# First layer of batch 0: weight halves ahead of x in the load queue, masked half 0 applied ahead of half 1's products

## The chip, the cores and the metric

One NeuronCore of a Trainium2 chip. The metric is device time in microseconds of one execution. The kernel before was timed in three runs: median 412.96 us, 412.57 to 413.46.

## The reference

Four sequences (batches) of 512 tokens with 256 features go through two layers with residuals.

```python
# layer 0: weights mixed per batch by cond (4 x 8), masked, applied
masked_w = weight * mask[None]                       # weight 8 x 256 x 256
w_bot = einsum('bg,got->bot', cond, masked_w)
x = x + einsum('bnt,bot->bno', x, w_bot) + bias
# layer 1: top 2 of 8 experts by softmax(cond), and a shared expert, each a gated MLP 256 -> 1024 -> 256
mlp(x) = (gelu(x @ gate) * (x @ up)) @ down
x = x + mlp_shared(x) + sum_k w_k * mlp_expert_k(x)
```

## The kernel before

Everything is held transposed: features on the 128 partitions (two halves, hh or oh), tokens along the free axis. Products of full precision are made from fp32r operands split in two: hi = the rounded value (a ScalarE copy), lo = the rest (a subtraction on VectorE or GpSimd, called POOL here), and three matmuls hi*hi, hi*lo, lo*hi.

A batch has 24 steps. Step s is one chunk of 128 hidden features: gate and up projection (`gate_up`, `project`, L524 to L562: twelve matmuls of 512 columns), then GELU on ScalarE (`activate`), the product on VectorE (`form_h`, L1044), and the splits of that. Two steps form a pair, whose down projection is done with seven block products instead of eight (L582); its operands are sums and differences t1 to t4 (`form_t1`, `form_t234`) and B12, copied on ScalarE (`copy_b12`). Steps 0 to 7 use the shared expert, 8 to 23 the two chosen ones. TensorE runs two steps ahead: while VectorE works on step s it projects step s + 2. The up projection of step s + 2 goes to the PSUM buffer of step s, so it waits for `split_b11` or the t parts of it (L557 to L562): for step 2 it waits until `h_lo_done` is 1, which is the first `split_b11` (L1080) behind the second `form_h`.

Ahead of that stands the prologue, in which batch 0 gets its first layer. The masked weights of an output half oh are a sum over g of cond[g] times l0_raw[:, oh, g]. Part of the eight products is made by VectorE (`combine_0`, L971, into l0_first), part by TensorE with a diagonal matrix holding cond[g] (`mix_l0`, L426, into PSUM; a plain fp32 matmul, recorded as two passes). VectorE adds the two (`add_mixed_0`, L980, and for half 1 `add_mixed_1`, L990, in two parts th), multiplies by the mask (L985, L996), ScalarE makes the hi part (L694, L698), VectorE the lo part (L1001, L1005). x enters p_ps through an identity matmul (`pass_x` with its hi part, `pass_x_rest` with its lo part), so that p_ps holds x plus the first layer; `first_layer_part` (L443) adds the weights' matmuls. When an output half of p_ps is complete (`l0_done`), ScalarE forms x1_hi (`first_x1_hi`, L755), VectorE x1_lo (`first_x1_lo`, L1014), and ScalarE later x1 itself (`first_x1`, L759). `keep_warm` (L651) issues matmuls on zeros.

The order of the work on every engine is written out by hand, at the end of its block: TensorE L660 to L681, ScalarE L891 to L926, VectorE L1190 to L1218, POOL in its `batch_0`, and SP's queue, which issues all loads, from L409. Engines run in their own order and wait for semaphores. On POOL, `batch_0` starts when half 1 is masked (`first_masked` at 3), then splits the first shared gate and up weights one after the other, then forms sums of the down weights (`form_s`, the last of its four at L1252), splits chunk 3 (L1233) and the down weights (L1262, L1264). Routing weights (`route_sums`, `route_weigh` at L957: a reciprocal L959, a tensor_tensor L961, a tensor_scalar L963, a scalar_tensor_tensor L965, all on 4 or 8 columns, each waiting for the one before) are VectorE's, between the splits of half 1 and the rests of x1.

The order of the loads is: weights 0 to 3 of half 0 (512 KB), all of x of batch 0 (512 KB), weights 4 to 7 of half 0, the mask with the bias (257 KB), weights 0 to 3 of half 1, weights 4, 5 and 6, 7 of half 1 (256 KB each), then the shared expert's weights.

Of the kernel before, what the change touches and what calls it, by code (L numbers as in the profile page):

```python
# [10 lines left out]
ACT = mybir.ActivationFunctionType  # L11
# [23 lines left out]
def build(nc, xT, cond, l0_w, l0_mask, experts, shared, outT):  # L35
# [22 lines left out]
    with ExitStack() as ctx:  # L58
# [90 lines left out]
        l0_in = [sem(f"l0_in{i}") for i in range(5)]  # L149
        mask_in = sem("mask_in")  # L150
        first_mixed = sem("first_mixed")
# [50 lines left out]

        DIAGS = (2, 3, 6, 7, 5)

# [52 lines left out]
        def chunks_at(s):  # L257

            if s == 1:
                return range(4, 5)  # L260
            if s == 3:
                return range(5, 7)
            if s == 5:
                return range(7, 10)
            return range(s + 3, min(s + 5, CHUNKS + ECH))
# [4 lines left out]
        def _(sp):  # L270
# [7 lines left out]
            def load_l0_last(i):  # L278
                at = slice(QUAD + 2 * i, QUAD + 2 * (i + 1))
                sp.dma_start(l0_raw[:, 1, at], l0_w[1, 1, :, bass.ds(2 * i * D, 2 * D)].rearrange("p (g d) -> p g d", d=D)).then_inc(l0_in[3 + i], 16)  # L280

            def load_x_0():
# [126 lines left out]
            sp.sem_inc(stored, 1)  # L409
            load_l0(0, 0)  # L410
            load_x_0()
            load_l0(0, 1)
            sp.dma_start(mask[:], l0_mask).then_inc(mask_in, 16)
            load_l0(1, 0)
            for i in range(2):
                load_l0_last(i)
            shared_weights()
            batch_0()
# [6 lines left out]
        def _(pe):  # L425
# [23 lines left out]
            def first_layer_0():  # L449

                pe.wait_ge(first_hi_done, 1)
                for th in range(HH):
                    first_layer_part(l0_hi, 0, th, x_hi)
                mix_l0(1, 5)
                mix_l0(1, 7, last=True)
                for th in range(HH):
                    first_layer_part(l0_hi, 0, th, x_lo)
                pe.wait_ge(first_lo_done, 1)
                for th in range(HH):
                    first_layer_part(l0_lo, 0, th, x_hi, last=(th == HH - 1))  # L460
                for th in range(HH):
                    pe.wait_ge(first_hi_done, 2 + th)
                    for x in (x_hi, x_lo):
                        first_layer_part(l0_hi, 1, th, x)
                for th in range(HH):
                    pe.wait_ge(first_lo_done, 2 + th)
                    first_layer_part(l0_lo, 1, th, x_hi, last=(th == HH - 1))
# [35 lines left out]
            def first_gate_up():  # L503

                w_hi, w_lo = gu_weights(0)
                for hh in range(HH):
# [5 lines left out]
                    for ps, off, lo_done in ((g_ps, GATE, part_lo_done), (u_ps[:, 0], UP, gu_lo_done)):  # L512
                        at = off + hh * P
                        pe.wait_ge(lo_done, 1)
                        pe.matmul(ps, w_lo[:, at:at + P], x1_at(x1_hi, 0, hh), start=False, stop=False)
                for ps, off, done in ((g_ps, GATE, g_done), (u_ps[:, 0], UP, u_done)):
                    for hh in range(HH):
                        if off == GATE:
                            pe.wait_ge(x1_lo_done, hh + 1)
                        at = off + hh * P  # L520
                        mm = pe.matmul(ps, w_hi[:, at:at + P], x1_at(x1_lo, 0, hh), start=False, stop=(hh == HH - 1))
                    mm.then_inc(done, 1)

# [141 lines left out]
            mix_l0(0, 3)  # L665
            pass_x(0)
            keep_warm(1)
            pass_x(1)
            mix_l0(0, 6)
            mix_l0(0, 7, last=True)  # L670
            pass_x_rest(0)
            mix_l0(1, 2, first=True)
            mix_l0(1, 3)
            pass_x_rest(1)
            first_layer_0()
# [8 lines left out]
        def _(act):  # L684
# [127 lines left out]
            def weights_beside(b, s):  # L812

                if at_first(b):
# [6 lines left out]
                    if s % 2 == 0 and 0 < s < CHUNKS:  # L821
                        split_shared_d(s // 2)
                        split_shared_s(s // 2)
                    if s >= CHUNKS and s % 2 == 0:
# [29 lines left out]
            def step(b, s, with_next):  # L854
                activate(b, s)
                if at_first(b) and s == 2:
                    for oh in range(HH):
                        first_x1(oh)
                if s % 2 == 0 and s > 0 and fast(b, s // 2 - 1):
# [4 lines left out]
                elif s % 2 == 0:  # L864
                    if at_first(b) and s == 2:
                        weights_beside(b, 1)
                    weights_beside(b, s)
                    copy_b12(b, s // 2)
                else:
                    split_b11(b, s // 2)  # L870
# [28 lines left out]
            for g in DIAGS[2:]:  # L899
                scale_ident(g)  # L900
            for hh in range(HH):
                split_x(0, hh)
            act.activation(gelu[:, 0, 0:8], shifted[:, 0], ACT.Gelu_apprx_tanh)
            split_l0_0()
            split_gate(0)
            split_up(0)
            for th in range(HH):
                split_l0_1(th)
            first_x1_hi(0)
            split_gate(1)  # L910
# [9 lines left out]
            split_b11(0, 0)  # L920
            split_shared_s(0)
            split_b2(0, 0)
            batch(0, True)
# [9 lines left out]
        def _(dve):  # L933
# [37 lines left out]
            def combine_0(oh, g, first=False):  # L971
# [4 lines left out]
                else:  # L976
                    dve.wait_ge(first_mixed, 4 * oh + {1: 1, 4: 2, 5: 3, 6: 3}[g])
                    dve.scalar_tensor_tensor(acc, w, cond_all[:, 0, g:g + 1], acc, ALU.mult, ALU.add).then_inc(first_mixed, 1)  # L978

            def add_mixed_0():  # L980
                dve.wait_ge(first_mixed, 4)
                dve.wait_ge(mixed, 1)
                dve.tensor_tensor(half(l0_first, 0), half(l0_first, 0), mix_ps[0], ALU.add).then_inc(first_added, 1)

            def apply_mask_0():  # L985
                dve.wait_ge(mask_in, 16)
                dve.wait_ge(first_added, 1)
# [8 lines left out]
            def apply_mask_1(th):  # L996
                at = slice(D + th * P, D + (th + 1) * P)
                dve.wait_ge(first_added, 2 + th)
                dve.tensor_tensor(l0_first[:, at], l0_first[:, at], mask[:, 1, th * P:(th + 1) * P], ALU.mult).then_inc(first_masked, 1)
# [193 lines left out]
            route_sums()  # L1193
            for hh in range(HH):
                first_x_lo(hh)
            combine_0(0, 4)
            combine_0(0, 5)
            add_mixed_0()
            apply_mask_0()
            combine_0(1, 0, first=True)  # L1200
            split_l0_0()
            combine_0(1, 1)
            combine_0(1, 4)
            combine_0(1, 6)
            for th in range(HH):
                add_mixed_1(th)
                apply_mask_1(th)
            for th in range(HH):
                split_l0_1(th)
            route_weigh()  # L1210
            for oh in range(HH):
                first_x1_lo(oh)
            route_index()
            for s in range(2):
                step(0, s, False)
            batch(0, True)
# [5 lines left out]
        def _(pool):  # L1222
# [74 lines left out]
            def batch_0():  # L1297
# [10 lines left out]
                for s in range(1, STEPS):  # L1308
                    if s % 2:
                        p = (s + 1) // 2  # L1310
                        if s in (3, 5):
                            split_shared(chunks_at(s)[0])
                        if p < PAIRS:
                            shared_s(p)
                        elif p < NP:
                            expert_s(0, p - PAIRS)
                        for c in chunks_at(s)[1 if s in (3, 5) else 0:]:
                            if c < CHUNKS:
# [94 lines left out]
```

## Time and profile before

| | |
|---|---|
| median of 3 runs | 412.96 us |
| profiled execution, its own time | 412.5 us |
| its span on the core | 410.7 us |
| TensorE busy | 405.5 us, 99% of the span, 2236 matmuls |
| TensorE weight loads busy | 352.7 us, 86% |
| VectorE | 306.8 us, 75% |
| ScalarE | 252.8 us, 62% |
| POOL | 313.2 us, 76% |
| granted TensorE clock | 1.0 |
| DMA | 35.23 MB, mean 86 GB/s |

The span is what the trace covers; the execution's time lies 1.8 us above it. In a row of the timeline the first number is the start in us from the span's beginning, the second the time from the first start to the last end of the instructions merged in it, then engine, line, operation, output <- inputs with shapes, the number of instructions, and in brackets how long the engine had stood idle and what released it. Names in the rows are shortened (l_raw is l0_raw, x_hi and x_lo can be x1_hi and x1_lo). PEld is the weight load ahead of a matmul, SPq the queue of SyncE. Ends of matmuls are modelled.

### The profile page before, as it was taken

To read this page: it belongs to the slowest core of one execution; us is meant where nothing else is said; L and a number is where in the kernel's file an instruction comes from. 1 tells how busy PE (TensorE), PEld (TensorE's weight loads), DVE (VectorE), ACT (ScalarE), POOL (GpSimd) and SP (SyncE) were. 2 spreads that over 40 slices of the span, in tenths; PEclk is the share of its full clock that TensorE was granted. 3 is DMA by queue.
4 is the path that set the end of the run, shared out by engine and by line. 5 is a ranking of instruction groups with operands and counts; after the bars stand their busy time and mean duration, and the time that the engine had idled before them with its cause. 6 is when DMAs were issued, how large, how long until landed. Compare 5 with 4: busy or idle time off the path is not lost.

```text
span 410.7 us, 7438 instructions
## 1 busy us (share of the span) xinstructions
PE 405.5 (99%) x2236; PEld 352.7 (86%) x2236; DVE 306.8 (75%) x516; ACT 252.8 (62%) x482; POOL 313.2 (76%) x322
## 2 busy tenths in 40 slices
PE   8999999999999999999999999999999999999997
PEld 5788888888888988888889888888888888888886
DVE  5778886586658887767677879857687677677784
ACT  5687677565565668555655666757455656676541
POOL 1699999999719689999635879999670977999630
PEclk9999999999999999999999999999999999999999
DMA  8543342333200622333000152222201042241101
GB/s 297 205 138 97 120 104 91 102 86 98 75 4 7 190 60 86 122 105 102 28 26 1 51 184 97 77 77 98 81 26 27 0 130 76 77 129 54 51 1 53
DMA packets 18895, 35.23 MB, mean 86 GB/s; under 512 B 2098, under 2 KB 2610, under 8 KB 18866
## 3 DMA queue, kind: packets, MB, share of 16 engines
q1 hardware_dynamic: 18576, 34.61, 26.7%
q8 instruction: 14, 0.23, 0.2%
q10 hardware_dynamic: 290, 0.26, 0.2%
q14 instruction: 15, 0.12, 0.1%
HBM read 32.77 MB, written 2.10 MB: 85 GB/s over the span
## 4 chain that ended last, share of the span: by engine, by line
PE 97%; DVE 2%; issue 0%; ACT 0%; POOL 0%; DVEq 0%; POOLq 0%
PE o_ps L582 16%; PE p_ps L582 12%; PE g_ps L528 11%; PE u_ps L527 11%; PE u_ps L531 10%; PE u_ps L528 10%; PE g_ps L527 10%; PE g_ps L531 10%; PE l_ps L481 2%; PE g_ps L653 1%; PE u_ps L430 1%; PE o_ps L622 0%; DVE t_raw L978 0%; DVE out_sb L1131 0%; DVE x_lo L1016 0%
## 5 line engine op out<-in xcount | busy, mean ns | idle before, releaser
L1237 POOL TENSOR_TENSOR eg_lo<-raw_g,eg_hi 128x512 fp32r<-128x512 f32 x64 | 92.5, 1468 | 11.1 <-ACT eg_hi L737 11.1
L766 ACT ACTIVATE gelu<-g_ps 128x512 f32<-128x512 f32 x95 | 56.9, 599 | 52.6 <-PE g_ps L531 50.9
L1054 DVE SCALAR_TENSOR_TENSOR u_ps<-gelu,route_cur,u_ps 128x512 f32<-128x512 f32 x64 | 48.1, 752 | 48.3 <-PE u_ps L531 45.0
L1090 DVE TENSOR_TENSOR h_lo<-t_raw,h_hi 128x1024 fp32r<-128x1024 f32 x46 | 81.3, 1766 | 0.5 <-ACT h_hi L799 0.5
L1279 POOL TENSOR_TENSOR ed_lo<-s_raw,ed_hi 128x512 fp32r<-128x512 f32 x30 | 54.6, 1821 | 0.0
L786 ACT CAST h_hi<-u_ps 128x256 fp32r<-128x256 f32 x46 | 17.2, 373 | 57.5 <-DVE t_raw L1069 42.4
L528 PE MATMUL g_ps<-x_hi,eg_lo 128*128 128x512 f32 (+1 forms) x128 | 50.2, 392 | 0.0
L527 PE MATMUL g_ps<-x_hi,eg_hi 128*128 128x512 f32 (+1 forms) x128 | 50.0, 391 | 0.0
L527 PE MATMUL u_ps<-x_hi,eg_hi 128*128 128x512 f32 (+1 forms) x128 | 49.8, 389 | 0.0
L528 PE MATMUL u_ps<-x_hi,eg_lo 128*128 128x512 f32 (+1 forms) x128 | 49.8, 389 | 0.0
L799 ACT CAST h_hi<-t_raw 128x1024 fp32r<-128x1024 f32 x46 | 47.9, 1040 | 0.4 <-DVE t_raw L1076 0.2
L1085 DVE TENSOR_TENSOR h_lo<-u_ps,h_hi 128x512 fp32r<-128x512 f32 x46 | 31.8, 692 | 17.5 <-ACT h_hi L793 17.5
L1277 POOL TENSOR_TENSOR ed_lo<-raw_d,ed_hi 128x384 fp32r<-128x384 f32 x30 | 33.5, 1118 | 13.4 <-ACT ed_hi L746 13.2
L531 PE MATMUL g_ps<-x_lo,eg_hi 128*128 128x512 f32 (+1 forms) x128 | 39.5, 390 | 0.0
L531 PE MATMUL u_ps<-x_lo,eg_hi 128*128 128x512 f32 (+1 forms) x128 | 39.4, 389 | 0.0
L737 ACT CAST eg_hi<-raw_g 128x512 fp32r<-128x512 f32 x64 | 36.6, 623 | 0.0
L1049 DVE TENSOR_TENSOR u_ps<-gelu,u_ps 128x512 f32<-128x512 f32 x32 | 22.2, 692 | 18.7 <-PE u_ps L531 18.0
L793 ACT CAST h_hi<-u_ps 128x512 fp32r<-128x512 f32 x46 | 27.0, 587 | 14.6 <-DVE u_ps L1054 7.3
L582 PE MATMUL o_ps<-h_hi,ed_hi 128*128 128x256 f32 x120 | 34.0, 283 | 0.0
L582 PE MATMUL o_ps<-h_lo,ed_hi 128*128 128x256 f32 x120 | 34.0, 283 | 0.0
L582 PE MATMUL o_ps<-h_hi,ed_lo 128*128 128x256 f32 x120 | 34.0, 283 | 0.0
L1351 POOL TENSOR_TENSOR out_sb<-x,x_in 128x512 f32<-128x512 f32 x6 | 7.6, 1295 | 32.9 <-DVE x L1096 32.9
(230 smaller groups left out, 1147.8 us busy)
## 6 DMA issues: line engine op xcount, KB each, us to landing
raw_g<-experts SPq DMA_DIRECT2D x64, 256.0 KB, 2.7
raw_d<-experts SPq DMA_DIRECT2D x32, 256.0 KB, 2.7
raw_g<-shared SPq DMA_DIRECT2D x8, 256.0 KB, 5.7
l_raw<-l_w SPq DMA_DIRECT2D x3, 512.0 KB, 5.8
x_in<-xT SPq DMA_DIRECT2D x6, 256.0 KB, 3.2
outT<-out_sb SPq DMA_DIRECT2D x6, 256.0 KB, 3.0
raw_d<-shared SPq DMA_DIRECT2D x4, 256.0 KB, 3.2
x_in<-xT SPq DMA_DIRECT2D x1, 512.0 KB, 4.2
```

Of the source, the lines that this page charges most:

```text
L527: pe.matmul(ps, w_hi[:, at:at + P], x1_at(x1_hi, b, hh), start=(hh == 0), stop=False)
L528: pe.matmul(ps, w_lo[:, at:at + P], x1_at(x1_hi, b, hh), start=False, stop=False)
L531: mm = pe.matmul(ps, w_hi[:, at:at + P], x1_at(x1_lo, b, hh), start=False, stop=(hh == HH - 1))
L582: mm = pe.matmul(ps, block_of(wt[w], blk), half_of((h_hi, h_lo)[h], hf), start=(first and i == 0), stop=(last and i == 2))
L737: act.copy(eg_hi[:, j % RING], raw_g[:, j % RAW_G]).then_inc(gu_hi_done, 1)
L766: act.activation(gelu[:, s % 2], l0_ps if at_first(b) and s == 1 else g_ps, ACT.Gelu_apprx_tanh).then_inc(gelu_done, 1)
L799: act.copy(h_hi[:, T1 * TH:7 * TH], t_raw[:]).then_inc(t_hi_done, 1)
L1054: dve.scalar_tensor_tensor(u_ps[:, s % 2], gelu[:, s % 2], route_cur[:, k:k + 1], u_ps[:, s % 2], ALU.mult, ALU.mult).then_inc(h_done, 1)
L1090: dve.tensor_tensor(h_lo[:, at], t_raw[:], h_hi[:, at].bitcast(F32), ALU.subtract).then_inc(t_lo_done, 1)
L1237: pool.tensor_tensor(eg_lo[:, j % RING], raw_g[:, j % RAW_G], eg_hi[:, j % RING].bitcast(F32), ALU.subtract).then_inc(gu_lo_done, 1)
L1277: pool.tensor_tensor(ed_lo[:, q % RING_D, 0:3 * P], raw_d[:, slot, 0:3 * P], ed_hi[:, q % RING_D, 0:3 * P].bitcast(F32), ALU.subtract)
L1279: pool.tensor_tensor(ed_lo[:, q % RING_D, S1 * P:7 * P], s_raw[:], ed_hi[:, q % RING_D, S1 * P:7 * P].bitcast(F32), ALU.subtract).then_inc ...
```

## The change

- Loads: weights 0 to 3 and 4 to 7 of half 0, then half 0 of the mask (with its bias column), then x, then weights of half 1, then half 1 of the mask. The mask has a semaphore for each half.
- Shares: of half 0's eight products TensorE makes g = 2, 3, 7 and VectorE 0, 1, 4, 5, 6 (before: 2, 3, 6, 7 and 0, 1, 4, 5). Of half 1's, TensorE makes 2, 3, 5, 6, 7 and VectorE 0, 1, 4 (before: 2, 3, 5, 7 and 0, 1, 4, 6).
- TensorE: three products of half 0, three warming matmuls (before one), both x parts; then masked half 0 times x_hi, the rest of x of half 0, one matmul with x_lo, products 2 and 3 of half 1, the lo weights of half 0, the rest of x of half 1, the last matmul of half 0, products 5, 6, 7 of half 1. In `first_gate_up` the matmuls with x1_lo of an hh follow those with x1_hi of the same hh.
- VectorE: five products of half 0, add, mask; x rest 0, lo part of half 0, x rest 1; half 1 as before with three products. `route_weigh` moves from ahead of the rests of x1 to between step 0 and step 1.
- ScalarE: the GELU table is loaded ahead of the x copies; the copy of up chunk 0 moves behind half 1's copies and `first_x1_hi(0)` ahead of them; `first_x1(0)` goes between the split of the shared down sums and `split_b2` of step 1, `first_x1(1)` into step 2 behind the split of chunk 4, chunk 5 follows; the split of the down sums of later pairs moves behind `copy_b12`.
- POOL: in the first steps chunk 4 is split ahead of the sums of pair 1 and chunk 5 behind them, chunk 6 follows in step 3.

```diff
-        DIAGS = (2, 3, 6, 7, 5)
+        DIAGS = (2, 3, 7, 6, 5)
...
             if s == 1:
-                return range(4, 5)
+                return range(4, 6)
             if s == 3:
-                return range(5, 7)
+                return range(6, 7)
...
+            def load_mask(oh):
+                sp.dma_start(mask[:, oh], l0_mask[:, oh]).then_inc(mask_in[oh], 16)
...
-            load_l0(0, 0)
+            for i in range(2):
+                load_l0(0, i)
+            load_mask(0)
             load_x_0()
-            load_l0(0, 1)
-            sp.dma_start(mask[:], l0_mask).then_inc(mask_in, 16)
             load_l0(1, 0)
             for i in range(2):
                 load_l0_last(i)
+            load_mask(1)
             shared_weights()
...
                 pe.wait_ge(first_hi_done, 1)
                 for th in range(HH):
                     first_layer_part(l0_hi, 0, th, x_hi)
-                mix_l0(1, 5)
-                mix_l0(1, 7, last=True)
-                for th in range(HH):
-                    first_layer_part(l0_hi, 0, th, x_lo)
+                pass_x_rest(0)
+                first_layer_part(l0_hi, 0, 0, x_lo)
+                mix_l0(1, 2, first=True)
+                mix_l0(1, 3)
                 pe.wait_ge(first_lo_done, 1)
                 for th in range(HH):
-                    first_layer_part(l0_lo, 0, th, x_hi, last=(th == HH - 1))
+                    first_layer_part(l0_lo, 0, th, x_hi)
+                pass_x_rest(1)
+                first_layer_part(l0_hi, 0, 1, x_lo, last=True)
+                mix_l0(1, 5)
+                mix_l0(1, 6)
+                mix_l0(1, 7, last=True)
...
-                for ps, off, done in ((g_ps, GATE, g_done), (u_ps[:, 0], UP, u_done)):
-                    for hh in range(HH):
-                        if off == GATE:
-                            pe.wait_ge(x1_lo_done, hh + 1)
+                    pe.wait_ge(x1_lo_done, hh + 1)
+                    for ps, off, done in ((g_ps, GATE, g_done), (u_ps[:, 0], UP, u_done)):
                         at = off + hh * P
                         mm = pe.matmul(ps, w_hi[:, at:at + P], x1_at(x1_lo, 0, hh), start=False, stop=(hh == HH - 1))
-                    mm.then_inc(done, 1)
+                        if hh == HH - 1:
+                            mm.then_inc(done, 1)
...
             mix_l0(0, 3)
-            pass_x(0)
-            keep_warm(1)
-            pass_x(1)
-            mix_l0(0, 6)
             mix_l0(0, 7, last=True)
-            pass_x_rest(0)
-            mix_l0(1, 2, first=True)
-            mix_l0(1, 3)
-            pass_x_rest(1)
+            keep_warm(3)
+            for hh in range(HH):
+                pass_x(hh)
             first_layer_0()
...
                 if at_first(b) and s == 2:
-                    for oh in range(HH):
-                        first_x1(oh)
+                    split_shared(4)
+                    first_x1(1)
...
             split_l0_0()
             split_gate(0)
-            split_up(0)
+            first_x1_hi(0)
             for th in range(HH):
                 split_l0_1(th)
-            first_x1_hi(0)
+            split_up(0)
...
             route_sums()
-            for hh in range(HH):
-                first_x_lo(hh)
-            combine_0(0, 4)
-            combine_0(0, 5)
+            for g in (4, 5, 6):
+                combine_0(0, g)
             add_mixed_0()
             apply_mask_0()
+            first_x_lo(0)
+            split_l0_0()
+            first_x_lo(1)
             combine_0(1, 0, first=True)
-            split_l0_0()
             combine_0(1, 1)
             combine_0(1, 4)
-            combine_0(1, 6)
...
-            route_weigh()
             for oh in range(HH):
                 first_x1_lo(oh)
             route_index()
-            for s in range(2):
-                step(0, s, False)
+            step(0, 0, False)
+            route_weigh()
+            step(0, 1, False)
             batch(0, True)
```

## Rows read from the trace of the kernel before

**Rows 1.** Waits of TensorE's weight loads, 18 to 411 us: us in total, times, longest.
```profile
PEld u_ps L527 <- issue: 0.3, 1, 0.3
```
**Rows 2.** Timeline of TensorE, 4 to 23 us.
```profile
4.54 1.91 PE L430 MATMUL u_ps<-l_raw,out_sb 128*128 128x256 f32 x4
...
7.71 1.20 PE L430 MATMUL u_ps<-l_raw,out_sb 128*128 128x256 f32 x4
...
9.66 1.10 PE L430 MATMUL u_ps<-l_raw,out_sb 128*128 128x256 f32 x4 [0.53 <-DMA l_raw<-l_w]
...
10.83 0.63 PE L445 MATMUL p_ps<-x_hi,l_hi 128*128 128x512 f32 x2
...
11.30 1.02 PE L430 MATMUL u_ps<-l_raw,out_sb 128*128 128x256 f32 x4
...
15.02 0.39 PE L511 MATMUL g_ps<-x_hi,sg_hi 128*128 128x512 f32 x1
...
18.27 0.40 PE L527 MATMUL l_ps<-x_hi,sg_hi 128*128 128x512 f32 x1
...
22.44 0.47 PE L527 MATMUL u_ps<-x_hi,sg_hi 128*128 128x512 f32 x1
```
**Rows 3.** Timeline of ScalarE and VectorE, 5 to 13 us.
```profile
5.53 1.14 ACT L692 CAST x_hi<-x_in 128x512 fp32r<-128x512 f32 x2
...
6.18 1.29 DVE L1012 TENSOR_TENSOR x_lo<-x_in,x_hi 128x512 fp32r<-128x512 f32 x2
...
7.59 1.07 DVE L978 SCALAR_TENSOR_TENSOR t_raw<-l_raw,cond_all,t_raw 128x256 f32<-128x256 f32 x2
...
9.01 0.42 DVE L983 TENSOR_TENSOR t_raw<-t_raw,u_ps 128x256 f32<-128x256 f32 x1 [0.35 <-PE u_ps L430]
...
10.00 0.41 ACT L696 CAST l_hi<-t_raw 128x256 fp32r<-128x256 f32 x1 [1.81 <-DVE t_raw L988]
...
12.47 0.29 DVE L994 TENSOR_TENSOR t_raw<-t_raw,u_ps 128x128 f32<-128x128 f32 x1
```
**Rows 4.** The mask's issue in SP's timeline, and its line of the DMA view, to 60 us.
```profile
2.25 0.43 SPq L413 DMA_DIRECT2D mask<-l_mask  x1
...
mask<-l_mask SPq DMA_DIRECT2D x1, 257.0 KB, 6.0
```
**Rows 5.** Timeline of POOL and VectorE, 14.3 to 16.1 us.
```profile
14.38 0.79 POOL L1229 TENSOR_TENSOR sg_lo<-raw_g,sg_hi 128x256 fp32r<-128x256 f32 x1
...
14.70 0.50 DVE L961 TENSOR_TENSOR pair<-probs,pair_rsum 128x8 f32<-128x8 f32 x1
...
15.13 0.74 POOL L1225 TENSOR_TENSOR sg_lo<-raw_g,sg_hi 128x256 fp32r<-128x256 f32 x1
...
15.23 0.67 DVE L963 TENSOR_SCALAR pair_rest<-pair 128x8 f32<-128x8 f32 x1
...
15.93 0.17 DVE L965 SCALAR_TENSOR_TENSOR route_w<-pair,pair_rest 128x8 f32<-128x8 f32 x1
```
**Rows 6.** Timeline of TensorE, VectorE and POOL, 17 to 22.5 us.
```profile
17.00 0.97 PE L521 MATMUL g_ps<-x_lo,sg_hi 128*128 128x512 f32 x2
...
17.47 0.19 PEld L521 LDWEIGHTS g_ps<-x_lo,sg_hi 128*128 128x128 f32 x1 [0.47 <-DVE x_lo L1016]
...
18.64 0.70 DVE L1049 TENSOR_TENSOR u_ps<-gelu,u_ps 128x512 f32<-128x512 f32 x1 [0.67 <-ACT gelu L766]
...
19.75 0.46 POOL L1252 TENSOR_TENSOR s_raw<-raw_d,s_raw 128x128 f32<-128x128 f32 x1
19.77 0.42 DVE L1069 TENSOR_TENSOR t_raw<-b,u_ps 128x256 f32<-128x256 f32 x1 [0.44 <-ACT b L780]
...
20.17 1.29 POOL L1233 TENSOR_TENSOR sg_lo<-raw_g,sg_hi 128x512 fp32r<-128x512 f32 x1
...
21.27 0.69 DVE L1049 TENSOR_TENSOR u_ps<-gelu,u_ps 128x512 f32<-128x512 f32 x1 [1.08 <-PE u_ps L531]
...
21.42 1.02 POOL L1262 TENSOR_TENSOR sd_lo<-raw_d,sd_hi 128x384 fp32r<-128x384 f32 x1
```

More of the change, by code:

```diff
@@ L149, in build @@
         l0_in = [sem(f"l0_in{i}") for i in range(5)]
-        mask_in = sem("mask_in")
+        mask_in = [sem(f"mask_in{oh}") for oh in range(HH)]
         first_mixed = sem("first_mixed")
@@ L822, in weights_beside @@
                         split_shared_d(s // 2)
-                        split_shared_s(s // 2)
                     if s >= CHUNKS and s % 2 == 0:
@@ L865, in step @@
                     if at_first(b) and s == 2:
-                        weights_beside(b, 1)
+                        split_shared(5)
                     weights_beside(b, s)
                     copy_b12(b, s // 2)
+                    if at_first(b) and s < CHUNKS:
+                        split_shared_s(s // 2)
                 else:
@@ L900, in _ @@
                 scale_ident(g)
+            act.activation(gelu[:, 0, 0:8], shifted[:, 0], ACT.Gelu_apprx_tanh)
             for hh in range(HH):
                 split_x(0, hh)
-            act.activation(gelu[:, 0, 0:8], shifted[:, 0], ACT.Gelu_apprx_tanh)
             split_l0_0()
             split_gate(0)
-            split_up(0)
+            first_x1_hi(0)
             for th in range(HH):
                 split_l0_1(th)
-            first_x1_hi(0)
+            split_up(0)
             split_gate(1)
@@ L921, in _ @@
             split_shared_s(0)
+            first_x1(0)
             split_b2(0, 0)
@@ L976, in combine_0 @@
                 else:
-                    dve.wait_ge(first_mixed, 4 * oh + {1: 1, 4: 2, 5: 3, 6: 3}[g])
+                    dve.wait_ge(first_mixed, 5 * oh + {1: 1, 4: 2, 5: 3, 6: 4}[g])
                     dve.scalar_tensor_tensor(acc, w, cond_all[:, 0, g:g + 1], acc, ALU.mult, ALU.add).then_inc(first_mixed, 1)
             def add_mixed_0():
-                dve.wait_ge(first_mixed, 4)
+                dve.wait_ge(first_mixed, 5)
                 dve.wait_ge(mixed, 1)
@@ L985, in apply_mask_0 @@
             def apply_mask_0():
-                dve.wait_ge(mask_in, 16)
+                dve.wait_ge(mask_in[0], 16)
                 dve.wait_ge(first_added, 1)
@@ L997, in apply_mask_1 @@
                 at = slice(D + th * P, D + (th + 1) * P)
+                dve.wait_ge(mask_in[1], 16)
                 dve.wait_ge(first_added, 2 + th)
@@ L1310, in batch_0 @@
                         p = (s + 1) // 2
-                        if s in (3, 5):
+                        if s in (1, 5):
                             split_shared(chunks_at(s)[0])
@@ L1316, in batch_0 @@
                             expert_s(0, p - PAIRS)
-                        for c in chunks_at(s)[1 if s in (3, 5) else 0:]:
+                        for c in chunks_at(s)[1 if s in (1, 5) else 0:]:
                             if c < CHUNKS:
```

## The prediction

> **What bounds the kernel now.** I read the waits of TensorE first. From 18 us to the end its weight loads waited once, 0.3 us, at the first up projection of shared chunk 2 (the row at L527) [rows 1]; with the 99% busy share of the table above that says the stretch behind the prologue is a solid stream of matmuls. So a microsecond counts only if it moves that stream's start, or opens a hole in it. I then read the timeline of TensorE and fixed three points in it [rows 2]: **H** = 10.83, the first matmul with the masked half 0 of the first layer's weights; **A** = 12.47, where VectorE adds the products of half 1 to its own sum [rows 3]; **U** = 22.44, the start of that up projection, L527. Behind U nothing waits, so the change is worth what it moves U. Between A and U everything hangs on A: first gate matmul A + 2.55 (15.02), second gate-up S = A + 5.80 (18.27), U = A + 9.97.
>
> **Transfers.** x, the second transfer, was there by 5.53, where ScalarE copies it, and weights 4 to 7 of half 0 (third) by 7.59, where VectorE's third product starts [rows 3]; the mask, 257 KB, landed at 2.25 + 6.0 = 8.25 [rows 4]. In the new order the second place, 5.5, belongs to weights 4 to 7, and x ends after 1664.5 KB instead of 1024. Between 1536 KB (7.59) and 1793 KB (8.25) that is 7.9. Bounds: 7.2 if each 256 KB costs 0.65 us behind 5.53, and 8.3 at the mask's landing. I take 7.9. The second mask transfer adds one issue on SP's queue (0.43 us for a mask issue [rows 4]), ahead of the shared weights; those wait for bytes in flight, and nothing reads them before the half 0 copy, so I count it as nothing (0.5 us of a landing if that cover were gone, before POOL needs it at A + 1.2).
>
> **Half 0.** VectorE is free by 6.18 and no longer turns to x there [rows 3]. Three products in a row at 0.59 each ((1.07 - 0.48) per step), then the add and the mask, behind which ScalarE's copy began 0.99 after the add (9.01 to 10.00) [rows 3]: 6.18 + 1.77 + 0.99 = 8.94, instead of 10.00. TensorE has only three products there, the last at 7.2 even at the slow pace of (1.91 - 0.63)/3 = 0.43 a pass, two passes each [rows 2]. But ScalarE now copies x ahead of it: two copies take 1.14 [rows 3], from 7.92, and the copy of half 0 follows at about 9.0. 0.41 for it [rows 3] and 0.05 to TensorE give H = 9.48, which is 1.35 earlier. Were x earlier, VectorE would still hold H at 9.4.
>
> **Half 1, where I expect the gain to turn into a loss.** In the old order four matmuls and two products lay between H and the join. In the new one TensorE issues, in order: two x parts, a rest of x, one part, two products, two parts, a rest, one part, and only then the last three products. That is eight matmuls of 512 columns at 0.23 (0.63 - 0.40) and ten product passes at (1.02 - 0.38)/3 = 0.21 [rows 2]: 1.88 + 2.15 = 4.03 us behind H. VectorE's add started 0.49 after the start of the last pass in the earlier join (7.71 + 1.20 - 0.38 = 8.53, to 9.01) [rows 2, 3], so A = 9.48 + 4.03 - 0.21 + 0.49 = 13.79. VectorE's own three products of half 1 would be through by about 12.1 (half 0 low part, rest of x, then 0.48 + 2 x 0.59 from 10.4), so its product moved to TensorE buys nothing. A moves by **+1.32**. Bounds: +1.2 for an x landed at 7.2, +1.7 at 8.3.
>
> **The first gate-up.** Before, the x1 rests came late: VectorE did the routing weights first, and TensorE stood 0.5 us for the second rest [rows 6]. Now route_weigh is behind step 0 and rests follow the split at once; TensorE runs its 12 matmuls unbroken from A + 2.55: S = A + 2.55 + 12 x 0.234 = A + 5.36, so **-0.44**. If the second rest were late after all the gain is at most lost: 0 to -0.44, and I take all of it: VectorE is free for the rests 1.5 us earlier (the routing weights held it from 14.6 to 16.1 [rows 5]) and the second one needs only the x1_hi copy ahead of it.
>
> **The moved routing weights.** They now stand between VectorE's t1 (L1069) and its second form_h, on whose split U waits: U came 1.17 behind form_h [rows 2, 6]. The last gate matmul is at A + 4.89; form_h(0) came 1.17 behind it, 0.11 of that a restart (the old one ran 17.47 to 17.97, 0.50, where a matmul in the stream takes 0.39), so A + 5.95, and t1 1.13 later, A + 7.08 [rows 6]. After its 0.33 step and a 0.17 reciprocal, L961 asks at A + 7.6. What does it meet? In its old place the four tiny instructions were not tiny [rows 5]: L961, two SBUF inputs, 8 columns, took 0.50 and ended at 15.20 as POOL's instruction of 14.38 did (15.17); L963 took 0.67 and ended at 15.90, as POOL's of 15.13 did (15.87). L965, with POOL idle, took 0.17. So each of the first two waited for one whole POOL instruction. POOL's queue hangs on A too: its instructions of 19.75, 20.17 and 21.42 [rows 6] end at A + 7.74, A + 8.99, A + 9.97. Then L961 gets in at A + 7.74, L963 at A + 8.99, L965 at A + 9.97, form_h(1) at A + 9.95 instead of S + 3.00 = A + 8.36, and U = A + 9.95 + 1.17 = A + 11.12: **+1.15** on A + 9.97, in which the 0.44 is already spent. L965's own wait is not shown by a row; bounds are 0 (as with POOL idle) and one POOL instruction, 1.0; I take 1.0, as it reads two SBUF tensors like L961.
>
> The Trainium skill (SBUF — State Buffer, "Who interferes with whom") says that a DVE instruction with two SBUF inputs, or in a two-port mode, fully blocks behind a GpSimd instruction that reads SBUF. By that rule L965 waits too and +1.15 stands; without it the term would be +0.3. The trace agrees for L961 and L963 [rows 5]; for L965 no row does.
>
> **The rest.** ScalarE's reordered copies around x1 and the split of the shared down weights fill time in which it waits for form_h(1), and POOL's earlier chunk 5 comes before anything needs it; TensorE never waited there, and a later U gives both more room. Nothing, against at most some tenths if a copy were late. Eight products on each of TensorE and VectorE stay eight; two more warming matmuls fall into the wait for x.
>
> **Sum.** U moves by 1.32 + 1.15 = +2.47. The profiled execution took 412.5 (span 410.7); it would take 415.0. The median of the runs is 0.46 above it, 412.96, so I forecast 415.4. About 0.2%, 0.83 us, is what a measurement can tell from no change here.
>
> **Rivals.**
> - POOL does not hold L961 to L965 in their new place (the starts miss one another): form_h(1) at A + 8.36, U = A + 9.53, total +1.32 - 0.44 = +0.88, 413.8. For it: many POOL instructions end close together. Against it: 1.29 and 1.02 us of POOL stand exactly there. 0.14. If L965 alone goes free, form_h(1) is at A + 9.1 and the total +1.6, 414.6: 0.12.
> - L961 misses the gap at A + 7.74, by 0.13 us in my sum, and all three slip one POOL instruction, the last then as long as L1233's 1.29 by estimate: form_h(1) A + 11.2, total +3.7, 416.7. 0.20.
> - **Faster**: TensorE's products of half 1 are not what ends last. Then VectorE's own sum decides, A = 12.07, and with the routing weights unheld U moves by -0.40 - 0.44 = -0.84, 412.1. It decides as soon as the last pass starts by 11.6, two microseconds ahead of my 13.3; TensorE's unbroken 4.03 us behind H speak against it, and H cannot fall to 7.8. 0.04.
> - TensorE, standing between 8.3 and 9.5 except for two passes of x, falls back to its 1.2 GHz pace (0.43 per 512 columns instead of 0.23): +3.8 us more, 419. Against: in the old kernel it stood most of 9.0 to 9.66 and came back fast [rows 2]. 0.03.
> - The change does what it says only for half 0, which lies off the path: that is the main case.
>
> **Numbers.** Main case 0.45; rivals 0.14, 0.12, 0.20, 0.04, 0.03; 0.02 for what I do not see. The range runs from below the unheld case with x early (413.6) to the missed gap with x at 8.3 (417.0), leaving out some 0.15. Faster by over 0.2% 0.04; within 0.2%, the low part of the unheld case, 0.10; slower 0.86.
>
> **What would show it.** Right: L696 ends near 9.4; the first L994 starts near 13.8 and is released by TensorE; L961, L963 and L965 take 0.1 to 1.3 us each and end with POOL's instructions; a hole of about 1.5 us ahead of the first L527 of chunk 2. Wrong: VectorE's own product releases the L994 add (no loss in half 1), or U less than 10.3 behind A (no hold), or new TensorE waits behind U.

## The result, and the profile after

The changed kernel takes 415.73 us (median of 8 runs, 415.47 to 418.79) against 413.0 for the kernel before on the same chip: ratio 1.0084, 95% interval 1.007 to 1.0097, so 2.7 us slower in the medians. The ratio of the medians is 1.0066, below that interval: two of the eight executions took 418.45 and 418.79 us, at a granted clock of 0.996 against 0.999 to 1.0 in the others, and are likely what lifts the recorded ratio. The forecast was 415.4, within 413.6 to 417.0, slower with 0.86.

The profiled execution took 416.29, span 414.4 against 410.7. Its page, first part:

```profile
span 414.4 us, 7445 instructions
PE 405.9 (98%) x2238; PEld 353.3 (85%) x2238; DVE 307.5 (74%) x516; ACT 252.8 (61%) x482; POOL 313.3 (76%) x322
```

Two more matmuls and not a microsecond more work on any engine: the 3.7 us are waiting. These are the waits of TensorE from 24 us to the end, first of its matmuls, then of its weight loads (columns as in [rows 1], which has the weight loads alone):

```profile
PE u_ps L535 <- DVE h_lo L1086: 1.5, 1, 1.5
```

```profile
PEld u_ps L535 <- issue: 1.9, 1, 1.9
PEld u_ps L535 <- DVE h_lo L1086: 0.3, 1, 0.3
```

The long one is at the first up projection of chunk 2 (L535 now, L527 before), which is U. Behind it the matmuls show no wait, but the weight loads show one, of 0.3 us, which [rows 1] does not have. So the time is again read from the three points, and that wait comes on top. The lines below answer to those of [rows 2] and [rows 3]: ScalarE's copies of x, its copy of half 0, H, TensorE's last products of half 1, A, S, U. The changed kernel, timeline, 8 to 26 us:

```profile
8.82 1.14 ACT L695 CAST x_hi<-x_in 128x512 fp32r<-128x512 f32 x2 [1.71 <-DMA x_in<-xT]
...
9.86 0.40 ACT L699 CAST l_hi<-t_raw 128x256 fp32r<-128x256 f32 x1
...
10.41 0.63 PE L449 MATMUL p_ps<-x_hi,l_hi 128*128 128x512 f32 x2
...
13.14 1.46 PE L434 MATMUL u_ps<-l_raw,out_sb 128*128 128x256 f32 x6
...
14.71 0.29 DVE L999 TENSOR_TENSOR t_raw<-t_raw,u_ps 128x128 f32<-128x128 f32 x1 [1.94 <-PE u_ps L434]
...
20.16 0.39 PE L535 MATMUL l_ps<-x_hi,sg_hi 128*128 128x512 f32 x1
...
25.91 0.47 PE L535 MATMUL u_ps<-x_hi,sg_hi 128*128 128x512 f32 x1 [1.51 <-DVE h_lo L1086]
```

U went from 22.44 to 25.91, 3.47 of the 3.7 us. The 0.2 that is left is the second wait of the weight loads, at the first up projection of chunk 4:

```profile
34.06 0.19 PEld L535 LDWEIGHTS u_ps<-x_hi,sg_hi 128*128 128x128 f32 x1 [0.26 <-DVE h_lo L1086]
```

The down projection behind it begins at 38.29, in the kernel before at 34.60: from here on the two streams are 3.69 to 3.71 apart, up to the end. The control below has the same wait (0.26 at 33.49). So have all other runs on the changed kernel, and before_pool_order, which is before_weigh_early with the changed order of chunks 4 and 5; before_weigh_early has not, nor has before_weigh_late, in which U came late as well. So the wait goes with that order on ScalarE and POOL, and not with the late U. Half 0 did get earlier, H from 10.83 to 10.41. But VectorE then stood 1.94 us for TensorE's last three products (the add, L999), and A came 2.24 later than before. S - A fell from 5.80 to 5.45, U - A rose from 9.97 to 11.20.

Where the second rise comes from is in the routing instructions, which answer to [rows 5]. The same timeline, POOL and VectorE:

```profile
22.14 0.46 POOL L1257 TENSOR_TENSOR s_raw<-raw_d,s_raw 128x128 f32<-128x128 f32 x1
...
22.23 0.17 DVE L964 RECIPROCAL pair_rsum<-pair_sum 128x4 f32<-128x4 f32 x1
...
22.44 0.18 DVE L966 TENSOR_TENSOR pair<-probs,pair_rsum 128x8 f32<-128x8 f32 x1
22.56 1.29 POOL L1238 TENSOR_TENSOR sg_lo<-raw_g,sg_hi 128x512 fp32r<-128x512 f32 x1
...
22.66 1.22 DVE L968 TENSOR_SCALAR pair_rest<-pair 128x8 f32<-128x8 f32 x1
...
23.80 1.01 POOL L1267 TENSOR_TENSOR sd_lo<-raw_d,sd_hi 128x384 fp32r<-128x384 f32 x1
23.91 0.92 DVE L970 SCALAR_TENSOR_TENSOR route_w<-pair,pair_rest 128x8 f32<-128x8 f32 x1
...
24.75 0.68 DVE L1055 TENSOR_TENSOR u_ps<-gelu,u_ps 128x512 f32<-128x512 f32 x1
```

An instruction on eight columns takes 1.22 us and ends at 23.88, where POOL's ended at 23.85; the next ends at 24.83, where POOL's ended at 24.81. The second form_h (24.75) stands behind both, though its up matmuls had been done since about 23.0.

### The profile page after: what moved, and what is told of

The parts are those of the page before. It is cut to its first block, busy times and chain, and to the rows that moved or that the text cites. A ratio compares the mean times of both kernels' runs of the same rounds, so it can differ in the third digit from the quotient of the medians.

```text
span 414.4 us, 7445 instructions
## 1 busy us (share of the span) xinstructions
PE 405.9 (98%) x2238; PEld 353.3 (85%) x2238; DVE 307.5 (74%) x516; ACT 252.8 (61%) x482; POOL 313.3 (76%) x322
## 4 chain that ended last, share of the span: by engine, by line
PE 95%; DMA 2%; DVE 1%; issue 0%; ACT 0%; SPq 0%; DVEq 0%
PE o_ps L590 16%; PE p_ps L590 12%; PE u_ps L535 10%; PE g_ps L536 10%; PE u_ps L536 10%; PE u_ps L539 10%; PE g_ps L535 10%; PE g_ps L539 10%; PE l_ps L490 2%; DMA x_in<-xT 2%; PE p_ps L449 1%; PE u_ps L434 1%; PE o_ps L630 0%; DVE u_ps L1055 0%; DVE out_sb L1137 0%
## 5 line engine op out<-in xcount | busy, mean ns | idle before, releaser
L1242 POOL TENSOR_TENSOR eg_lo<-raw_g,eg_hi 128x512 fp32r<-128x512 f32 x64 | 91.5, 1452 | 11.1 <-ACT eg_hi L740 11.1
L1284 POOL TENSOR_TENSOR ed_lo<-s_raw,ed_hi 128x512 fp32r<-128x512 f32 x30 | 53.7, 1790 | 0.0
L535 PE MATMUL g_ps<-x_hi,eg_hi 128*128 128x512 f32 (+1 forms) x128 | 50.0, 391 | 0.0
L535 PE MATMUL u_ps<-x_hi,eg_hi 128*128 128x512 f32 (+1 forms) x128 | 49.8, 389 | 0.0
L1282 POOL TENSOR_TENSOR ed_lo<-raw_d,ed_hi 128x384 fp32r<-128x384 f32 x30 | 34.5, 1150 | 13.2 <-ACT ed_hi L749 12.9
```

Of the source, the lines that this page charges most:

```text
L535: pe.matmul(ps, w_hi[:, at:at + P], x1_at(x1_hi, b, hh), start=(hh == 0), stop=False)
L1242: pool.tensor_tensor(eg_lo[:, j % RING], raw_g[:, j % RAW_G], eg_hi[:, j % RING].bitcast(F32), ALU.subtract).then_inc(gu_lo_done, 1)
L1282: pool.tensor_tensor(ed_lo[:, q % RING_D, 0:3 * P], raw_d[:, slot, 0:3 * P], ed_hi[:, q % RING_D, 0:3 * P].bitcast(F32), ALU.subtract)
L1284: pool.tensor_tensor(ed_lo[:, q % RING_D, S1 * P:7 * P], s_raw[:], ed_hi[:, q % RING_D, S1 * P:7 * P].bitcast(F32), ALU.subtract).then_inc ...
```

## The experiments

Every run is on the changed kernel unless it says "the kernel before". Since x lands at a different time in every execution, the readings are distances: A - H (the join of half 1), S - A, U - A. In the table H is the first matmul of masked half 0, ratios are against the kernel before on the same chip (its medians there: 412.5 to 412.9). Medians of different runs were partly taken on different chips.

| run | median us | ratio (95%) | H | A - H | S - A | U - A |
|---|---|---|---|---|---|---|
| kernel before | 412.5 to 413.0 | | 10.83 | 1.64 | 5.80 | 9.97 |
| changed kernel | 415.73 | 1.0084 (1.007 to 1.0097) | 10.41 | 4.30 | 5.45 | 11.20 |
| after_again | 415.74 | 1.0086 (1.0067 to 1.0106) | 9.82 | 4.30 | 5.46 | 11.21 |
| weigh_old_place | 415.2 | 1.0063 (1.0046 to 1.008) | 10.11 | 4.29 | 6.46 | 10.63 |
| weigh_in_x_wait | 414.61 | 1.0062 (1.0039 to 1.0085) | 9.41 | 4.49 | 5.45 | 9.61 |
| weigh_psum | 414.55 | 1.0052 (1.0035 to 1.0069) | 9.82 | 4.30 | 5.45 | 9.61 |
| before_weigh_late (kernel before) | 413.72 | 1.0018 (1.0005 to 1.0032) | 11.20 | 2.01 | 5.46 | 11.09 |
| products_first | 414.26 | 1.0033 (1.0017 to 1.0049) | 10.04 | 2.90 | 5.57 | 11.24 |
| share_four | 415.13 | 1.0058 (1.0041 to 1.0075) | 9.59 | 3.85 | 5.41 | 11.20 |
| x_second | 416.94 | 1.0102 (1.0085 to 1.0119) | 10.17 | 4.40 | 5.45 | 11.20 |
| after_combo | 413.36 | 1.0016 (1.0008 to 1.0025) | 9.79 | 3.14 | 5.54 | 10.13 |
| before_weigh_early (kernel before) | 412.81 | 1.0003 (0.9992 to 1.0013) | 10.84 | 1.59 | 5.31 | 9.46 |
| before_pool_order (kernel before) | 412.57 | 0.9989 (0.998 to 0.9998) | 11.37 | 2.01 | 5.29 | 9.45 |

### The control: after_again

> The changed kernel once more, unedited, as the control for the others and for where x lands. In its first profile x landed at 8.8 us, A (first L999, the add of half 1) was 14.71 and U (first L535 of chunk 2, up) 25.91, in an execution 0.6 us above the median. If the late x was that execution's own, x lands at 7.9 to 8.2 here, A is 13.8 to 14.1, and U - A stays 11.2. If it belongs to the new order of the loads, x lands at 8.6 or later again.

Close to the first case: x landed at 8.2, A was 14.12, U 25.33. The distances repeat to 0.01. Over the eight profiled executions with the new load order x's first copy starts between 7.8 and 8.8; the first profile had the latest.

### Routing weights: weigh_old_place, weigh_in_x_wait, weigh_psum, before_weigh_late

weigh_old_place:

```diff
+            route_weigh()
             for oh in range(HH):
                 first_x1_lo(oh)
             route_index()
             step(0, 0, False)
-            route_weigh()
             step(0, 1, False)
```

> The changed kernel with the routing weights (route_weigh) back ahead of the rests of x1. A unchanged. Theory (POOL holds the four tiny instructions, and in the new place they stand ahead of the form_h that U waits for): the rests come 1.5 us later, TensorE waits about 0.8 us in the first gate-up, U - A falls from 11.2 to about 10.4: 0.8 us faster than the changed kernel. Rival (the move is harmless, the loss is all in the half 1 join and the loads): U - A stays 11.2 or grows, 0 to 0.8 us slower than the changed kernel.

weigh_in_x_wait:

```diff
             apply_mask_0()
+            route_weigh()
             first_x_lo(0)
...
             step(0, 0, False)
-            route_weigh()
             step(0, 1, False)
```

> The changed kernel with the routing weights in VectorE's wait for x (behind the mask of half 0), where POOL is idle. Theory: each of the four takes under 0.2 us there, A is unchanged, the second form_h comes as soon as its up matmuls are done and U - A falls from 11.2 to 9.6: 1.6 us faster than the changed kernel. Rival (the hole ahead of U has another cause, ScalarE's reordered copies say): U - A stays above 10.5.

The edit of weigh_psum, which moves no instruction:

```diff
-        pair_rsum = sb("pair_rsum", [P, B])
-        pair = sb("pair", [P, B, TOP_K])
...
+        pair_rsum, pair = o_ps[:, 0, 0:B], o_ps[:, 0, 8:8 + B * TOP_K].rearrange("p (b k) -> p b k", k=TOP_K)
```

> The changed kernel with the same four instructions in the same place, but pair and the reciprocal of its sum in PSUM (in a bank not used yet), so that none of the four has two SBUF tensor inputs and the tensor_scalar reads PSUM. If it is the second SBUF input, or the tensor_scalar's SBUF source, that makes them wait for POOL, each takes under 0.3 us beside POOL's instructions and U - A falls to about 9.6, 1.6 us faster. If they wait for anything else (a queue, their place), they stay at 0.9 to 1.2 us and U - A at 11.2.

And on the kernel before, only the step loop around route_weigh:

```diff
-            route_weigh()
             for oh in range(HH):
                 first_x1_lo(oh)
             route_index()
-            for s in range(2):
-                step(0, s, False)
+            step(0, 0, False)
+            route_weigh()
+            step(0, 1, False)
```

> The kernel before with one part of the change: the routing weights between step 0 and step 1. A stays 12.47. Theory: the rests of x1 come early and the second gate-up starts 0.35 earlier, but POOL then holds the weights ahead of the second form_h, U - A grows from 9.97 to about 11.1: 1.1 us slower than before. Rival (the move gains what it was meant to): U - A 9.5 to 9.6, 0.4 us faster.

weigh_psum decides what the wait of these instructions hangs on. Its timeline (line numbers are one lower there; pair and its reciprocal are recorded as o_ps):

```profile
21.86 0.17 DVE L965 TENSOR_TENSOR o_ps<-probs,o_ps 128x8 f32<-128x8 f32 x1
21.97 1.30 POOL L1237 TENSOR_TENSOR sg_lo<-raw_g,sg_hi 128x512 fp32r<-128x512 f32 x1
22.07 0.17 DVE L967 TENSOR_SCALAR pair_rest<-o_ps 128x8 f32<-128x8 f32 x1
22.27 0.17 DVE L969 SCALAR_TENSOR_TENSOR route_w<-o_ps,pair_rest 128x8 f32<-128x8 f32 x1
```

The same instructions beside the same POOL instruction take 0.17 each once the tensor_scalar reads PSUM and the last one has a single SBUF input. U - A is 9.61, as it is when the instructions run in the wait for x with POOL idle (0.17 each there too). So both runs agree with the theory: 1.6 us of U - A. The kernel before with that one move shows the reverse: U - A up by 1.12, 1.1 expected, with its time up by 0.8; that its A came at 13.21 and not at 12.47 has another reason (last section). weigh_old_place goes the way of the theory, by 0.58 of U - A instead of 0.8: TensorE waited 0.70 for the first rest of x1, and the routing weights, in their old place, took 0.50 and 0.67 for the two middle ones exactly as in [rows 5].

But the time of weigh_in_x_wait fell by 1.1 and not by 1.6, though U - A did as expected. One part is that A was not unchanged: A - H grew from 4.30 to 4.49. The four instructions stand ahead of VectorE's rests of x, and the first of these began 1.41 behind ScalarE's first copy of x instead of 0.65. So U - H fell by 1.41. The other part lies behind U:

```profile
26.62 1.40 DVE L1096 TENSOR_TENSOR h_lo<-t_raw,h_hi 128x1024 fp32r<-128x1024 f32 x1 [0.52 <-ACT h_hi L802]
...
26.90 1.44 POOL L1253 TENSOR_TENSOR s_raw<-raw_d 128x128 f32<-128x128 f32 x1
...
28.84 0.46 POOL L1257 TENSOR_TENSOR s_raw<-raw_d,s_raw 128x128 f32<-128x128 f32 x1
...
29.34 0.62 ACT L731 CAST sd_hi<-s_raw 128x512 fp32r<-128x512 f32 x1 [1.56 <-POOL s_raw L1257]
...
29.96 0.59 ACT L769 ACTIVATE gelu<-g_ps 128x512 f32<-128x512 f32 x1
...
30.70 0.47 PE L535 MATMUL g_ps<-x_hi,sg_hi 128*128 128x512 f32 x1 [0.35 <-POOL sg_lo L1238]
```

TensorE stands about half a microsecond at the gate projection of chunk 4. The row names POOL's split, but that step needs the GELU of step 3, which ended at 30.55; ScalarE was late with it because it had stood 1.56 us at the copy of the down sums, for POOL's L1257. POOL was late in turn because its second sum (L1253, 26.90) took 1.44, where the ones beside it take 0.46 and 0.47: it ran beside VectorE's split of 1024 columns (26.62, two SBUF inputs, 1.40) and ended after it. So here, as the rows suggest, it is VectorE that holds POOL; no run takes this apart. In the changed kernel ScalarE stands there too (1.07 us, again for L1257), and the 1.5 us hole at U hides all of it but the 0.2 of above. Removing one hole uncovers the next: from U to the end of the span it is 389.0 us in both runs, against 388.5 in the changed kernel, and that half microsecond is given back. weigh_psum, where A - H is 4.30, has the same stop (30.93) and gained 1.2 us of time out of 1.6.

### The join of half 1: products_first, share_four, x_second

products_first, in `first_layer_0` and in ScalarE's order:

```diff
-                pass_x_rest(0)
-                first_layer_part(l0_hi, 0, 0, x_lo)
                 mix_l0(1, 2, first=True)
                 mix_l0(1, 3)
+                mix_l0(1, 5)
+                mix_l0(1, 6)
+                mix_l0(1, 7, last=True)
+                pass_x_rest(0)
+                first_layer_part(l0_hi, 0, 0, x_lo)
                 pe.wait_ge(first_lo_done, 1)
...
                 first_layer_part(l0_hi, 0, 1, x_lo, last=True)
-                mix_l0(1, 5)
-                mix_l0(1, 6)
-                mix_l0(1, 7, last=True)
...
-            first_x1_hi(0)
             for th in range(HH):
                 split_l0_1(th)
+            first_x1_hi(0)
             split_up(0)
```

> The changed kernel with TensorE's five products of half 1 right behind the first two matmuls of half 0, ahead of the six others (ScalarE copies half 1 ahead of x1_hi of half 0, so that it doesn't stand in its way). Theory (the join of half 1 waits for TensorE's queue behind H): the add comes six matmuls, 1.4 us, earlier against H, but TensorE still has those six to do before it can use half 1, so the first matmul with half 1 comes 0.9 us earlier against H (about H + 4.4 instead of H + 5.4) and the kernel is 0.8 to 1.0 us faster than the changed one. Rival (VectorE's own products or the loads set A): no change.

share_four:

```diff
-                mix_l0(1, 6)
...
             combine_0(1, 4)
+            combine_0(1, 6)
```

> The changed kernel with product 6 of half 1 back on VectorE. Theory: TensorE's queue behind H is one product, 0.43 us, shorter, VectorE has 1.9 us to spare for its 0.59: A 0.43 earlier against H (H + 3.87), 0.4 us faster. Rival (VectorE is the later one): A up to 0.6 later.

x_second:

```diff
-            for i in range(2):
-                load_l0(0, i)
-            load_mask(0)
+            load_l0(0, 0)
             load_x_0()
+            load_l0(0, 1)
+            load_mask(0)
```

> The changed kernel with the loads in the order of before: x second, weights 4 to 7 third, half 0 of the mask behind them; all orders of work on the engines as changed. Theory: x is there by 5.5 but VectorE's products 4, 5, 6 can begin only at 7.6, so H is at about 10.8 as before the change, and TensorE's 4 us behind it make A = H + 4.3 = 15.1, U = A + 11.2: slower than the changed kernel by 0.4 to 1.2 us. Rival (the late x is what costs): A returns to 12.5 to 13 and most of the loss is gone, 1.5 us faster than the changed kernel.

The two queue experiments move A as the queue says: four instead of five products, A - H 3.85 instead of 4.30 (0.45, 0.43 expected; 0.6 us of time, 0.4 expected); the products ahead of the six other matmuls, 2.90 (1.40, 1.41 by six times 0.23). The second gained 1.4 to 1.5 us (U - H 14.14 instead of 15.51; the medians differ by 1.5), more than the 0.8 to 1.0 expected: I had let half 1's copy be late against the rest of the queue, and it was not. TensorE began half 1's first matmul at 14.05, right behind half 0's last of 13.82. TensorE in products_first:

```profile
10.04 0.63 PE L449 MATMUL p_ps<-x_hi,l_hi 128*128 128x512 f32 x2
10.51 2.32 PE L434 MATMUL u_ps<-l_raw,out_sb 128*128 128x256 f32 x10
...
12.94 0.29 DVE L999 TENSOR_TENSOR t_raw<-t_raw,u_ps 128x128 f32<-128x128 f32 x1 [0.55 <-PE u_ps L434]
```

Even so VectorE waits for TensorE (0.55). In x_second ScalarE's copies of x start 1.2 us earlier than in the control (7.0, behind its table load), and it is the slowest of all: median 416.94, ratio 1.0102. VectorE's products 4 to 6 waited for their weights instead, and H + 4.4 made A 14.57. (Expected were H 10.8 and A 15.1; weights 4 to 7 landed at 7.0 there and not at 7.6.) So going back to the old load order does not take the loss away, and by the medians the new one is worth 1.2 us to this order of work (the intervals of the two ratios overlap, so its size is open). What lengthened the way from H to the join is that TensorE does 4 us of work there which the kernel before had done, in good part, before H, while it waited.

### Repairs: after_combo, before_weigh_early, before_pool_order

after_combo is weigh_in_x_wait, products_first and share_four together. before_weigh_early puts the four instructions one by one between VectorE's rests of x and products of half 0, and takes over the changed order of the rests in `first_gate_up`. before_pool_order adds to it:

```diff
             if s == 1:
-                return range(4, 5)
+                return range(4, 6)
             if s == 3:
-                return range(5, 7)
+                return range(6, 7)
...
                     if at_first(b) and s == 2:
-                        weights_beside(b, 1)
+                        split_shared(4)
                     weights_beside(b, s)
                     copy_b12(b, s // 2)
+                    if at_first(b) and s == 2:
+                        split_shared(5)
...
-                        if s in (3, 5):
+                        if s == 5:
                             split_shared(chunks_at(s)[0])
...
-                        for c in chunks_at(s)[1 if s in (3, 5) else 0:]:
+                        for c in chunks_at(s)[1 if s == 5 else 0:]:
```

> The changed kernel with the three repairs together: routing weights in the wait for x, half 1's products right behind the first two matmuls of half 0, four products of half 1 on each engine. Theory: now VectorE's four products set A at about H + 3.1 (instead of H + 4.3), U - A 9.6, so U about H + 12.7, with H at 9.4 to 10: U 22.1 to 22.7 and a time within 0.3 us of the kernel before, 2.8 us faster than the changed kernel. Rival (the late x costs by itself, whatever the queues do): over 1 us slower than before.

> The kernel before, with its loads and shares, the four routing instructions one by one between VectorE's rests of x and products of half 0 (POOL idle, TensorE's products later than VectorE's there), and the changed kernel's order of the rests of x1 in the first gate-up. Theory: A stays at 12.5 (or wherever its loads put it), U - A falls from 9.98 to 9.6: 0.37 us faster than before, 412.5, ratio 0.999, hardly clear of noise by time, clear in the trace. Rival (four more instructions delay the half 0 join): A later by up to 0.4 and nothing gained.

> The kernel of the run before_weigh_early, in which U came 0.55 us earlier than before the change but the gate-up of chunk 4 or 5 then stood for POOL's split of chunk 5; now POOL splits chunk 5 right behind chunk 4, ahead of the down weights of pair 1, and ScalarE copies it in step 2 behind copy_b12. Theory: the 0.4 to 0.55 us that were given back there are kept: no wait of TensorE behind U, 412.3, ratio 0.9987 to 0.9990. Rival: the next thing is late (GELU of step 3 behind ScalarE's extra copy, or the down weights) and it stays at 412.8.

after_combo takes back 2.4 us of the loss and stays 0.55 us (0.16%) behind, more than the 0.3 expected: A - H is 3.14 as expected, but U - A 10.13, half a microsecond over the 9.6. 0.09 of that is in S - A, where a weight load waited for POOL's split of up chunk 0. The rest is at the second form_h, which began 1.15 behind the start of the last two up matmuls instead of 0.72 as in weigh_in_x_wait; what held it is open. before_weigh_early gained U (21.89 instead of 22.44) and no time. Its timeline:

```profile
30.49 1.29 POOL L1241 TENSOR_TENSOR sg_lo<-raw_g,sg_hi 128x512 fp32r<-128x512 f32 x1 [0.47 <-ACT sg_hi L719]
...
31.84 0.50 PE L526 MATMUL g_ps<-x_hi,sg_hi 128*128 128x512 f32 x1 [0.34 <-POOL sg_lo L1241]
```

TensorE stands for POOL's split of chunk 5. In the kernel before that split ended at 31.56 and TensorE took it up at 31.89: 0.33 us of slack, and an earlier U was worth no more than that. With chunk 5 ahead of the down weights on POOL no matmul of TensorE waits behind 18 us any more, though weight loads still do three times (0.3, 0.3 and 0.2). The ratio is 0.9989 (0.998 to 0.9998), where 0.9987 to 0.9990 was expected: before_pool_order is ahead of the changed kernel, and of the kernel before by a tenth of a per cent, which is barely clear of no change. The trace says the same: U - A is 0.52 shorter than before, and from U to the end it is 0.4 us longer. Its profiled execution was the slowest of its eleven (413.3), with half 0 late at 11.37 (last section).

## Why the prediction held

- **Transfers**: 7.9 for x, within 7.2 to 8.3. Measured 8.8 in the first profile, beyond the upper end, 8.2 in the control, within it, and 7.8 to 8.8 over the eight profiles. The term was too small by 0.3 to 0.9 in the two profiles of this kernel. Interpolating by bytes had no place for a slow microsecond ahead of x (see the last section).
- **Half 0**: ScalarE's copy behind its two copies of x, as said: x + 1.05 to its start, H = x + 1.6. The step held, its input did not: 9.48 against 9.82 and 10.41. VectorE was a little earlier than in the sum: its masked half was ready at 8.60 in the control and not at 8.9, which the wait for x hid.
- **Half 1**: 4.03 us of queue behind H and A = H + 4.31. Measured 4.30 in both profiles, released by TensorE. This was the core of the loss, and share_four and products_first move it by the terms it was made of. A itself was 14.12 and 14.71 instead of 13.79, by the late x.
- **First gate-up**: S = A + 5.36, measured 5.45 (the first gate matmul came at A + 2.69, taken as A + 2.55; the rest of the way ran unbroken); weigh_old_place shows the 1.0 us that the early rests are worth with this order of matmuls (S - A 6.46), where I had counted 0.44 against the old order.
- **Routing weights**: U = A + 11.12, measured 11.20. The tensor_tensor (L961 before, L966 now) slipped in ahead of POOL's long instruction as said, in 0.18 us, the next two took 1.22 and 0.92. The wait of the scalar_tensor_tensor, which no row of before showed, is now shown: its upper bound was right. The Trainium skill (SBUF — State Buffer, "Who interferes with whom") says that a DVE instruction with two SBUF inputs contends with a GpSimd instruction that reads SBUF. The trace agrees: 0.92 with both inputs in SBUF, 0.17 with one of them in PSUM.
- **The rest at nothing**: nearly right. It cost 0.2 us, the wait of the weight load at 34.06, and "new TensorE waits behind U" was one of the signs of being wrong. The prediction had the wait in its upper bound ("some tenths") but not in its sum. It stayed that small because the hole at U covered the rest; without the hole it cost half a microsecond more (weigh_in_x_wait, weigh_psum).
- **Sum**: U moved 2.89 in the control (22.44 to 25.33) against 2.47 forecast; the medians moved 2.7. The difference in U is the landing of x (0.33 in A) and 0.08 behind A. With the 0.2 behind U the terms missed 0.6 us of the control. That the medians show 0.3 of it is luck: the profile of before lay 0.46 under its median, the control's only 0.14. Of the rivals, the missed gap and the unheld instructions did not occur, nor, in the two profiles, the slow clock: granted clock 0.999 and 1.0, 512 columns at 0.23 from H on. In the executions without a profile it may have. Three of the twelve of the changed kernel show a granted clock of 0.996 or 0.997 and took 418.45, 418.79 and 416.8 us, while all other executions on record that list a clock, 60 of them of the kernel before, show 0.998 to 1.0. A lower clock is what this rival, held at 0.03, would leave; no profile shows where those executions lost their time.

## What to carry to other kernels

When an operand is moved later in the load queue, write down what an in-order engine did while it waited for the other operands: that work now stands behind the arrival, and on this kernel 4 us of TensorE's queue ended up between the first masked half and the join of the second. Tiny VectorE instructions with two SBUF inputs, and the tensor_scalar on SBUF, belong where POOL is idle, or need an input in PSUM; beside POOL's instructions of 1.0 to 1.3 us they took 0.92 and 1.22 here instead of 0.17. The reciprocal of one SBUF input took 0.17 beside POOL as well. And before an earlier start is bought, read the slack of the next consumer (0.33 us here): beyond it the gain is taken back.

## What the runs showed that I had not expected

The half mask, 128 rows of 1028 bytes, in third place of the queue, goes with a dip in what the DMA engines move. The microsecond 5 to 6 of the changed kernel and of before_weigh_late, whose mask is whole and behind (columns: us, busy of PE, PEld, DVE, ACT, POOL, PEclk, DMA share, GB/s):

```profile
5.00:6.00 1.00, 1.00 (x4) 0.82 (x3) 0.90 (x6) 0.98 (x4) 0.00 (x0) 1.00 0.89 167
```

```profile
5.00:6.00 1.00, 1.00 (x4) 0.82 (x3) 0.81 (x5) 1.00 (x5) 0.00 (x0) 1.00 1.01 410
```

All eight profiles with the new load order show 167 to 239 there, the other five 352 to 410, among them x_second with the same half mask one place later (389). By estimate, near 200 GB/s missing for one microsecond, out of 400, is about half a microsecond of x's landing, and my interpolation lacked 0.3 to 0.9. The match is loose: 182 and 227 go with an x at 8.2 and 8.5, 239 with one at 7.8. Whether the size of the rows or their place makes the dip, and whether it is the mask's at all, was not tried.

The landing of x varies from execution to execution by up to 1 us with the new order (7.8 to 8.8) and by 0.3 with the old one (5.5 to 5.8, in the four profiles of the kernel before and its variants). With the old one A varies even so: 12.47, 12.43, 13.21 and 13.38. There it is TensorE's pace. These are two products of half 0, four passes, in before_weigh_early and in before_pool_order:

```profile
7.71 1.10 PE L430 MATMUL u_ps<-l_raw,out_sb 128*128 128x256 f32 x4
```

```profile
7.98 1.84 PE L430 MATMUL u_ps<-l_raw,out_sb 128*128 128x256 f32 x4
```

In the second a pass takes the slow 0.4 us and not 0.2, and VectorE's add stood 0.91 us for it; in before_weigh_late the four took 1.70 and the add stood 1.06. The granted clock reads 1.00 in these stretches of both, so the profile's clock column does not show the change of pace this early in the span; what set it is not shown. A change of 0.1% in this prologue is read from distances in the trace or from many runs, not from one time.
